# Last stage of a graph attention kernel: max(z, 0) and the residual are added before the exponential is there

## What is computed

```python
seq = (x @ W_seq).reshape(N, H, DH)
scores = leaky_relu(score1[:, :, None] + score2[:, None, :])
attn = softmax(scores + (1.0 - adj)[None] * MASK_VAL)
hidden = einsum('hij,jhd->ihd', attn, seq).reshape(N, D_IN)
z = hidden @ W_out + b_out
y = x + elu(z)                     # elu(z) = max(z, 0) + exp(min(z, 0)) - 1
out = (y - mean(y)) / sqrt(var(y) + 1e-5)
```

## Time and profile before

| | us |
|---|---|
| median of 3 runs | 536.79 (535.57 to 541.14) |
| the profiled execution, whole | 535.22 |
| its span, first to last instruction | 533.2 |
| last stage: first bias (L939) to first instruction of the last store | 467.22 to 530.62 |
| busy over the span: PE / DVE / ACT / POOL | 511.1 / 454.8 / 443.6 / 32.2 |

### The profile page before, as it was taken

The page is one execution under the profiler, slowest core; times in us unless marked ns, Lnnn a source line. Parts: engine busy times, 40 slices in busy tenths (PEclk is TensorE's granted clock), DMA queues, the critical chain, the costliest instruction groups (busy, mean ns, idle before and its releaser), DMA issues.

```text
span 533.2 us, 15405 instructions
## 1 busy us (share of the span) xinstructions
PE 511.1 (96%) x6805; PEld 462.6 (87%) x6805; DVE 454.8 (85%) x565; ACT 443.6 (83%) x485; POOL 32.2 (6%) x64
## 2 busy tenths in 40 slices
PE   8999998699999999999999999999999999799993
PEld 6888878599999999999999999999999999554542
DVE  3243988868889899999999999999998879888886
ACT  2677785889999999999999999999995989256664
POOL 3000000000000000000000000000000000025442
PEclk9999999889999999999999999999999999999997
DMA  7999992220210202022020210202112030014443
GB/s 272 363 354 332 364 247 48 82 81 2 82 47 36 80 2 81 3 80 81 3 81 2 80 52 33 82 2 80 39 45 81 2 139 2 1 59 146 131 139 118
DMA packets 30434, 52.76 MB, mean 99 GB/s; under 512 B 18336, under 2 KB 19616, under 8 KB 26400
## 3 DMA queue, kind: packets, MB, share of 16 engines
q1 hardware_dynamic: 29816, 51.26, 29.0%
q10 hardware_dynamic: 552, 0.52, 0.3%
HBM read 43.25 MB, written 4.33 MB: 89 GB/s over the span
## 4 chain that ended last, share of the span: by engine, by line
PE 81%; DVE 7%; ACT 6%; issue 3%; DMA 3%; ACTq 0%; DVEq 0%; POOLq 0%; POOL 0%
PE sums L440 40%; PE bank L456 22%; PE sums L514 10%; PE sums L363 6%; ACT tring L570 4%; DVE tring L736 2%; DMA adj<-tring 2%; DMA Vp<-in_L_gnn_W_seq_dram 1%; PE bank L502 1%; DVE tring L731 1%; PE sums L348 1%; DVE Vp L718 1%; DVE tring L713 1%; DVE xp L806 0%; ACT Vp L598 0%
## 5 line engine op out<-in xcount | busy, mean ns | idle before, releaser
L570 ACT ACTIVATE tring<-abc,ab 128x2048 int8<-128x2048 f32 x150 | 292.1, 2022 | 0.0
L440 PE MATMUL sums<-Vp,tring 128*128 128x132 f16 x4096 | 245.1, 222 | 10.6 <-DVE tring L736 7.5
L440 PEld LDWEIGHTS sums<-Vp,tring 128*128 128x128 fp8e4 x4096 | 239.2, 98 | 13.8 <-DVE tring L736 8.9
L736 DVE TENSOR_TENSOR tring<-adj,tring 128x1024 uint32<-128x1024 uint32 (+1 forms) x134 | 156.3, 1173 | 21.0 <-ACT tring L570 16.3
L456 PE MATMUL bank<-Vp,adj 128*128 128x132 f16 x2048 | 125.9, 221 | 0.0
L456 PEld LDWEIGHTS bank<-Vp,adj 128*128 128x128 fp8e4 x2048 | 122.3, 96 | 0.0
L731 DVE TENSOR_SCALAR tring<-abc,ab 128x2048 int8<-128x2048 f32 x90 | 115.4, 1282 | 0.0
L363 PE MATMUL sums<-Vp,abc 128*128 128x272 f32 x256 | 61.5, 393 | 0.0
L514 PE MATMUL sums<-abc,Vp 128*128 128x512 f32 (+1 forms) x136 | 57.5, 568 | 0.3 <-ACT Vp L663 0.3
L363 PEld LDWEIGHTS sums<-Vp,abc 128*128 128x128 f32 x256 | 47.3, 190 | 8.7
L514 PEld LDWEIGHTS sums<-abc,Vp 128*128 128x128 f32 x136 | 24.7, 190 | 22.9 <-issue 22.0
(11 more groups left out here) (96 smaller groups left out, 311.8 us busy)
## 6 DMA issues: line engine op xcount, KB each, us to landing
Vp<-in_adj_dram SPq DMA_DIRECT2D x16, 1024.0 KB, 8.0
abc<-a_rows SPq DMA_DIRECT2D x15, 1024.0 KB, 4.6
abc<-in_x_dram SPq DMA_DIRECT2D x16, 256.0 KB, 6.1
Vp<-in_x_dram SPq DMA_DIRECT2D x16, 256.0 KB, 2.9
out_dram<-Vp SPq DMA_DIRECT2D x16, 256.0 KB, 2.2
abc<-in_L_gnn_W_out_dram SPq DMA_DIRECT2D x1, 1024.0 KB, 5.2
Vp<-in_L_gnn_W_seq_dram SPq DMA_DIRECT2D x2, 256.0 KB, 5.1
Vp<-in_L_gnn_W_seq_dram ACTq DMA_DIRECT2D x2, 256.0 KB, 5.9
```

Source lines behind the costliest of these rows:

```text
L440: mm = pe.matmul(bank[b][:, c * 2 * VW:(c + 1) * 2 * VW], slot(jt)[:, it * P:(it + 1) * P].bitcast(F8), Vp[:, h, jt, :, :], start=(jt == 0 ...
L570: return act.activation(slot(jt)[:, columns], row(h)[:, columns], ACT.Sign, bias=ab[:, jt, H + h:H + h + 1], scale=-1.0)
L736: return dve.tensor_tensor(words, edges, words, ALU.bitwise_and)
```

## The change

elu(i) is split. A new operation, lift(i), makes yt = max(z, 0) + x and stands directly behind the bias of tile i, ahead of statistics(i-1) and hidden(i+3). It takes over the wait for out_ready of tile i-2 and the one for xr_loaded. What stays in elu(i) is one operation, yt = (e - 1) + yt. The count of operations is the same. ScalarE's wait for elu_ready becomes one for y_ready of the same tile. For the last tile, the left half's lift stands between its bias and statistics(14), the right half's behind its bias.

```diff
@@ scalar
                 if i >= 2:
-                    act.wait_ge(elu_ready, i - 1)
+                    act.wait_ge(y_ready, i - 1)
@@ vector
+            def lift(i, c, n):
+                r = i % 2
+                dve.wait_ge(z_ready, n)
+                if i >= 2:
+                    dve.wait_ge(out_ready, i - 1)
+                dve.wait_ge(xr_loaded[r], 16 * (i // 2 + 1))
+                dve.scalar_tensor_tensor(out=yt[:, r, c], in0=zt[:, r, c], scalar=0.0, in1=xr[:, r, c],
+                                         op0=ALU.max, op1=ALU.add).then_inc(lifted, 1)
             def elu(i, c, n):
                 r = i % 2
                 dve.wait_ge(e_ready, n)
-                if i >= 2:
-                    dve.wait_ge(out_ready, i - 1)
-                dve.scalar_tensor_tensor(out=yt[:, r, c], in0=zt[:, r, c], scalar=0.0, in1=et[:, r, c],
-                                         op0=ALU.max, op1=ALU.add).then_inc(elu_ready, 1)
-                dve.wait_ge(elu_ready, n)
-                dve.wait_ge(xr_loaded[r], 16 * (i // 2 + 1))
-                dve.scalar_tensor_tensor(out=yt[:, r, c], in0=yt[:, r, c], scalar=-1.0, in1=xr[:, r, c],
+                dve.wait_ge(lifted, n)
+                dve.scalar_tensor_tensor(out=yt[:, r, c], in0=et[:, r, c], scalar=-1.0, in1=yt[:, r, c],
                                          op0=ALU.add, op1=ALU.add).then_inc(y_ready, 1)
@@ rounds 0 to 14
                 bias(i, slice(0, D), bank[i % 2], i + 1)
+                lift(i, slice(0, D), i + 1)
                 if i > 0:
                     statistics(i - 1)
@@ last tile
             bias(i, left, made0, NT)
+            lift(i, left, NT)
             statistics(i - 1)
             bias(i, right, made1, NT + 1)
+            lift(i, right, NT + 1)
```

More of the change, by code:

```diff
@@ L202, in gat_kernel @@
         shift_ready, out_last = sem("shift_ready"), sem("out_last")
-        z_ready, zneg_ready, e_ready, elu_ready, y_ready = (sem(s) for s in ("z_ready", "zneg_ready", "e_ready", "elu_ready", "y_ready"))
+        z_ready, zneg_ready, e_ready, lifted, y_ready = (sem(s) for s in ("z_ready", "zneg_ready", "e_ready", "lifted", "y_ready"))
         stats_ready, mv_ready, v_eps, rstd_ready, out_ready = (sem(s) for s in ("stats_ready", "mv_ready", "v_eps", "rstd_ready", "out_ready"))
```

## The result

| | before | after |
|---|---|---|
| median, first comparison (5 runs each) | 536.79 | 542.51 |
| median, second comparison (19 and 4 runs) | 536.09 | 544.11 |
| first bias to final operation, profiled executions | 62.82 | 70.62 |

The changed kernel is slower: 1.0126 times the time of before, 95% interval 1.0082 to 1.0171; in the second comparison 1.0142, interval 1.0084 to 1.0200. The medians themselves lie 5.7 us apart in the first comparison and 8.0 in the second. The prediction was 545.0 us, range 541.5 to 549.5, slower.

A forecast was written before the change was run, and what follows sets the result against it. TensorE, 3.88 us a tile, was taken to bound the kernel; a 4.55 us cycle would replace it. Being 9.79 us late less 0.44 in the tail adds 9.35 to 535.2: 544.6, predicted as 545.0, range 541.5 to 549.5.

The forecast's parts named there:

- The cycle of one round through out_ready: Last stage: lift, previous tile's statistics, aggregation, GpSimd, ScalarE's output, next lift; claimed to replace TensorE's 3.87 us with 4.55 a round.
- the prediction's signs: Expected in the changed profile: VectorE waits about 1 us for L683 before the lift, rounds 3 to 14; middle biases 4.55 apart.
- The period: Middle rounds of the last stage: 0.62 lift to statistics, 3.90 statistics to output, 0.03 to next lift; 4.55 us together.
- what GpSimd runs beside stays the same: Middle rounds: VectorE's work beside GpSimd was taken as unchanged up to the end of L1030, then the bias replaces L950.
- the leg of 3.90: From the start of one tile's statistics through GpSimd to the end of ScalarE's output; 3.90 us, expected to carry over.
- The rule on the shared reads: VectorE instructions with two SBUF inputs contend with GpSimd's SBUF reads, others don't; gain below 0.1 us a round, left out.
- ScalarE's end to the lift's start: In each round, the step from the end of ScalarE's output to VectorE's next lift; taken as 0.03 us.
- The beginning: Biases 0 and 1 up to statistics(1) in the last stage; statistics(1) claimed to start 1.37 us late.
- Rounds 13 and 14: The rounds without hidden: statistics to output taken as 3.50 us, between 3.18 and 3.90, and a period of 4.15.
- From statistics(14) to the final operation: The tail: 4.92 us before the change, less 0.44 for one operation lost between exponential and statistics in the last half.
- TensorE's idle time: Each round, TensorE was to idle 0.68 us ahead of its turn, busy 3.87 of 4.55 us, 85%.
- The transfer: Rival: the residual's load, issued behind the store of tile i-2, binds the rounds; about 551 us, chance 0.03.

## Why the prediction was right, and by how much its terms missed

- **The cycle of one round through out_ready** was right, and so were its place and its direction: the lift waits for L683, TensorE is out of the chain, and its clock is 1.00 in every window up to 530 us. The waits are 14; the prediction's signs named rounds 3 to 14, and tiles 2 and 15 wait as well. It was shown by taking away the buffers' limit, by moving the lift alone, and by halving the lift.
- **The period, 4.55 forecast, 4.42 measured**, is the term that was mis-sized; over eleven rounds it is 1.4 us of the 1.55 by which the last stage's forecast of 9.35 us exceeded the measured 7.80. The step that failed is "what GpSimd runs beside stays the same", so that the leg of 3.90 carries over. It was 3.72. Before, L946 started 0.04 behind the end of ScalarE's exponential (484.69 and 484.73): 0.69 behind hidden, not 0.57 to 0.58 as L955 now, whose exponential is long there. The view of the waits had no entry for it because VectorE was busy almost up to that start. GpSimd's second operation ends about 0.42 behind that vector operation, so 0.11 of the leg was a wait for the exponential. I had the two rows side by side and did not subtract them. The prediction also says that L1030 took 0.57 in round 13 "with VectorE idle beside it". VectorE was idle only at its start: L1030 runs from 519.36 to 519.93, and L946, with two SBUF inputs, starts at 519.58. What counts is what VectorE does when the GpSimd operation starts.
- **The rule on the shared reads** (the Trainium skill, SBUF — State Buffer, Who interferes with whom) agrees with this case's runs in both halves: 0.86 us beside the added operation with two SBUF inputs, 0.56 beside the one with one. L1041 beside the bias took 0.27 where L1033 beside L950 took 0.34, 0.07 a round, inside the 0.1 that the prediction gave for the rule and left out of its sum. Together with the 0.11 this is the leg's 0.18.
- **ScalarE's end to the lift's start** was 0.09 and not 0.03, 0.06 a round the other way. VectorE does start 0.03 to 0.04 behind the exponential where it waits for that, but 0.08 to 0.10 behind L683 in every kernel where the lift waits for it, however long it had idled. Why is not shown.
- **The beginning**: statistics(1) 1.37 us late by the forecast, 1.27 by the profiles (9.53 less 8.26 behind the first bias). **Rounds 13 and 14**: leg 3.50 forecast, 3.45 and 3.42 measured. **From statistics(14) to the final operation** 4.48 forecast (4.92 less 0.44), 4.47 measured. The operation that this stretch lost is the left half's lift, which now stands ahead of statistics(14), behind a wait of 1.68 us for the output of tile 13; the right half's lift still stands in it.
- **TensorE's idle time** was seen where it was expected, ahead of its turn, waiting for hidden, and its clock did not fall. It was less than forecast: busy 13.69 of 15 us is 91%, where the prediction had 85%.
- **The transfer** did not bind, as forecast, but it was nearer than 0.03 sounds: as soon as rounds were shorter, with four yt buffers, it cost 0.11 us a round (3.98 against 3.87).
- **The whole time**: the ratios put the loss at 6.8 and 7.6 us (0.0126 and 0.0142 of the medians before); the last stage lost 7.80. The forecast of 545.0 lies 2.5 above the first median and 0.9 above the second. That it is so near is in part luck: the terms were 1.55 us too many, but the sum starts from the profiled execution of 535.22, which is 1.57 below the median of before. With the measured 7.80 on top of 536.79 it would also be 544.6.

## What to carry to other kernels

An operation that writes to a buffer takes the buffer's release wait with it. Before moving it up, ask whether the release depends on something queued behind it on the same engine; if it does, the move closes a cycle, and its period is the operation's own time plus the whole way round. Here 0.61 us of work inside a cycle of 3.8 us cost 0.55 us in each round, while the wait alone at the same place cost nothing. Either leave the operation behind what releases the buffer, or give more buffers, to the transfers that it now needs earlier as well; here it took four of each in place of two.

## What the runs showed of the hardware

GpSimd's second operation (L1030, L1038 and its like) on 128x1 operands took 0.56 to 0.57 us when it started with VectorE idle, even if a vector operation with two SBUF inputs began while it ran. When it started during such an operation, it ended 0.40 to 0.44 us behind that operation whatever followed, and so took 0.59 to 1.08 us, longer the more of that operation was left. When it started during an operation with one input from SBUF and one from PSUM, or during bn_stats, it took 0.56 to 0.57. These are all 208 such operations of the thirteen profiles. So the order of VectorE's operations, not their sum, set the length of GpSimd's part of the chain.
